# Two cross-attention blocks on one Trainium2 core: the last group's layer-1 probabilities turned by TensorE instead of VectorE and transfers

## What is computed

```python
q = (query @ Wq + bq).reshape(B, S, 16, 16).transpose(0, 2, 1, 3)
k = (key @ Wk + bk);  v = (value @ Wv + bv)          # one key/value head of 16
probs = softmax(where(|i - j| <= 64, q @ k.T * scale, NEG))
attn = (probs @ v) as (B, S, D) @ Wo + bo
gate = silu(concat([attn, query]) @ Wg + bg)
out = attn * gate + query * (1.0 - gate)
x_hat = out * rsqrt(mean(out * out, -1) + EPS) * rms_w
return x_hat - mean(x_hat, axis=1)
```

## Time and profile before

| | us |
|---|---|
| time, median of 3 runs (lowest to highest) | 1825.16 (1825.07 to 1828.34) |
| the profiled execution: its time | 1826.95 |
| the profiled execution: its span, first to last instruction | 1825.2 |
| PE busy in the span | 1792.8 (98%) |
| scores of group 31 start | 1785.96 |
| last `ag_sum` starts | 1813.90 |

### The profile page before, as it was taken

How to read it: one execution, slowest core, us unless ns; L and a number is a source line. 1 busy time by engine, 2 the same in 40 slices (tenths; PEclk the granted TensorE clock), 3 DMA queues, 4 the chain that set the end, 5 groups by cost and what they waited for, 6 DMA issues and landing times.

```text
span 1825.2 us, 55273 instructions
## 1 busy us (share of the span) xinstructions
PE 1792.8 (98%) x18702; PEld 1650.3 (90%) x18702; DVE 1485.3 (81%) x6755; ACT 1535.3 (84%) x5586; POOL 1292.3 (71%) x1324
## 2 busy tenths in 40 slices
PE   6999999999999999999999999999999999999997
PEld 5989999999999999999999999999999999999985
DVE  7878888888888888888888888888888888878775
ACT  5788888888889888889888889888888888888874
POOL 3656777767777766777766777776777776777754
PEclk9999999999999999999999999999999999999998
DMA  7434445444545544445544445444454444445432
GB/s 235 124 95 116 126 122 127 122 113 114 128 118 131 121 113 114 126 119 131 121 114 114 123 121 128 121 118 112 123 124 124 121 121 112 119 118 122 103 89 59
DMA packets 238059, 219.11 MB, mean 120 GB/s; under 512 B 48848, under 2 KB 220240, under 8 KB 237776
## 3 DMA queue, kind: packets, MB, share of 16 engines
q1 hardware_dynamic: 237776, 215.57, 47.2%
HBM read 71.29 MB, written 9.96 MB: 45 GB/s over the span
## 4 chain that ended last, share of the span: by engine, by line
PE 90%; DVE 4%; ACT 2%; POOL 1%; DMA 1%; issue 1%; SPq 0%; POOLq 0%; DVEq 0%; ACTq 0%
PE bank L616 11%; PE bank L618 11%; PE bank L617 11%; PE bank L630 9%; PE bank L634 8%; PE bank L631 8%; PE bank L790 7%; PE bank L803 7%; PE bank L915 4%; PE bank L928 3%; PE bank L626 3%; PE bank L622 3%; PE bank L623 3%; PE bank L640 2%; DVE soft L1754 1%
## 5 line engine op out<-in xcount | busy, mean ns | idle before, releaser
L2600 ACT ACTIVATE soft<-soft,row_min 128x128 f32<-128x128 f32 x1024 | 397.3, 392 | 60.9 <-DVE row_min L1754 60.8
L2520 ACT ACTIVATE soft<-soft,row_min 128x128 f32<-128x128 f32 x1024 | 398.5, 393 | 17.1 <-DVE row_min L1646 16.6
L3049 POOL TENSOR_TENSOR soft<-soft,inv_sum 128x512 f32<-128x512 f32 x256 | 271.4, 1061 | 145.7 <-DVE inv_sum L1654 145.7
L239 DVE STREAM_TRANSPOSE turned<-soft 128x512 f32<-128x512 f32 x512 | 341.8, 689 | 10.8 <-POOL soft L3058 4.7
L3058 POOL TENSOR_TENSOR soft<-soft,inv_sum 128x512 f32<-128x512 f32 x256 | 263.9, 1042 | 60.8 <-DVE inv_sum L1763 60.7
L1754 DVE CUSTOM_DVE_ANT_0 soft<-bank,winb 128x128 f32<-128x128 f32 x1024 | 230.3, 283 | 39.0 <-PE bank L915 36.3
L1646 DVE CUSTOM_DVE_ANT_0 soft<-bank,relb 128x128 f32<-128x128 f32 x1024 | 230.0, 281 | 15.3 <-PE bank L803 5.5
L2600 ACT ACTIVATION_READ_ACCUMULATOR soft<-soft,row_min 128x1 f32 x1024 | 195.2, 191 | 0.0
L2520 ACT ACTIVATION_READ_ACCUMULATOR soft<-soft,row_min 128x1 f32 x1024 | 195.0, 190 | 0.0
L790 PE MATMUL bank<-kT,qT 64*128 64x128 f32 x2048 | 148.7, 285 | 0.7 <-DVE kT L1626 0.7
L616 PE MATMUL bank<-wv,cT 128*128 128x256 f32 x512 | 146.5, 286 | 0.0
(11 more groups left out here) (249 smaller groups left out, 6448.5 us busy)
## 6 DMA issues: line engine op xcount, KB each, us to landing
soft<-turned SPq DMA_DIRECT2D x1024, 128.0 KB, 2.7
tokens<-stats_by_row SPq DMA_DIRECT2D x63, 256.0 KB, 3.6
tokens<-in_x SPq DMA_DIRECT2D x32, 256.0 KB, 2.8
raw<-in_x_t SPq DMA_DIRECT2D x32, 256.0 KB, 3.2
x<-in_x SPq DMA_DIRECT2D x32, 256.0 KB, 2.8
out<-gate SPq DMA_DIRECT2D x63, 128.0 KB, 2.5
tokens<-in_ctx SPq DMA_DIRECT2D x31, 256.0 KB, 2.9
raw<-in_ctx_t SPq DMA_DIRECT2D x31, 256.0 KB, 2.7
```

The lines of the kernel that those rows point to most:

```text
L239: return eng.transpose(turned[:, slot, :, s % 2, :, :].rearrange("p j h b -> p h j b"), soft[:, s, :, :].rearrange("p h (j a) -> p h j a", ...
L2520: last = act.activation(soft[:, s, h, :], soft[:, s, h, :], ACT.Exp, bias=row_min[:, s, h:h + 1], scale=-1.0, accum_out=row_sum[:, s, h:h ...
L2600: last = act.activation(soft[:, s, h, :], soft[:, s, h, :], ACT.Exp, bias=row_min[:, s, h:h + 1], scale=-1.0, accum_out=row_sum[:, s, h:h ...
L3049: pool.tensor_tensor(soft[:, m % NS0, :, :], soft[:, m % NS0, :, :], inv_sum[:, m % NS0, :].unsqueeze(2).broadcast_to([P, QUAD, SEQ]), ALU ...
```

## The change

Only group 31 (`g == NG - 1`) is touched. `norm1` writes its result into `turned`, with the keys in the order (a j) instead of (j a), so each write goes 16 bytes further than the one before, and no longer in place; for sequence 1 it waits until `turn_p` has read the same part for sequence 0. `turn_p` (PE) transposes the four heads of a unit with the identity into a bank; `place1` (DVE) copies the bank to the pair of slots, after both units of the pair are normalized. The eight `turn1` and the four `spread1` (16 transfers) go. PE's list is written anew with these calls in it, and other banks; `keep_busy` goes from 44 calls to 16 ahead of the turns and from 12 to 8 ahead of the last centering. `times_z`, `times_gate`, `plus_x` and `x_hat_lo` of sequence (31,1) go from POOL to DVE; `x_hat_lo(31,0)` on POOL moves ahead of `rrms_(31,1)`, and `y_out(31,0)` on DVE ahead of `x_hat(31,1)`.

```diff
@@ sync_program @@
-            spread1(NG - 1, 0, 0)
-            spread1(NG - 1, 0, 1)
-            spread1(NG - 1, 1, 0)
             store(NG - 2, 1)
-            spread1(NG - 1, 1, 1)
@@ tensor_program @@
+            def turn_p(g, b, u, bank, *drains):
+                freed(till, *drains)
+                till.wait_ge("norm1", unit1(g, b, u) + 1)
+                for h in range(QUAD):
+                    last = pe.transpose(bank[:, h * SEQ:(h + 1) * SEQ], in_key_order(u)[:, h, :], ident[:])
+                last.then_inc(sem["turn_p"], 1)
...
-                till.wait_ge(f"spread1_{n}", 16 * NB * (GROUP * g + b + 1))
+                if g == NG - 1:
+                    till.wait_ge("place1", NU1 * b + 2 * n + 2)
+                else:
+                    till.wait_ge(f"spread1_{n}", 16 * NB * (GROUP * g + b + 1))
...
-            keep_busy(banks[4], 44, ("min1", 8 * NG - 7))
...
+            keep_busy(banks[4], 16, ("min1", 8 * NG - 7))
+            turn_p(NG - 1, 0, 0, banks[4], ("min1", 8 * NG - 7))
+            turn_p(NG - 1, 0, 1, banks[1], ("min1", 8 * NG - 6))
+            pv1(NG - 1, 0, 0, banks[5], ("min1", 8 * NG - 3))
+            turn_p(NG - 1, 0, 2, banks[6], ("min1", 8 * NG - 5))
+            turn_p(NG - 1, 0, 3, banks[2], ("min1", 8 * NG - 4))
+            pv1(NG - 1, 0, 1, banks[5])
+            center_out(NG - 2, 1, banks[3], ("min1", 8 * NG - 2))
+            out_mm(NG - 1, 0, banks[7], ("min1", 8 * NG - 1))
+            turn_p(NG - 1, 1, 0, banks[4], ("place1", 1))
+            turn_p(NG - 1, 1, 1, banks[1], ("place1", 2))
+            out_mm_lo(NG - 1, 0, banks[7])
+            pv1(NG - 1, 1, 0, banks[0], ("min1", 8 * NG))
+            turn_p(NG - 1, 1, 2, banks[6], ("place1", 3))
+            turn_p(NG - 1, 1, 3, banks[2], ("place1", 4))
+            pv1(NG - 1, 1, 1, banks[0])
+            out_mm(NG - 1, 1, banks[4], ("place1", 5))
+            out_mm_lo(NG - 1, 1, banks[4])
+            keep_busy(banks[5], 8, ("o1_lo", 2 * NG - 1))
+            center_out(NG - 1, 0, banks[5], ("o1_lo", 2 * NG - 1))
+            center_out(NG - 1, 1, banks[3], ("y_out", 2 * NG - 2))
@@ vector_program @@
+            def place1(g, b, u, bank):
+                till.wait_ge("turn_p", NU1 * b + u + 1)
+                till.wait_ge("norm1", unit1(g, b, u | 1) + 1)
+                dve.tensor_copy(pair_of_slots(u // 2 if beside(g, b) else 2 + u // 2)[:, :, u % 2, :, :],
+                                bank[:].rearrange("p (h i b) -> p i h b", h=QUAD, i=NB)).then_inc(sem["place1"], 1)
...
-            turn1(NG - 1, 0, 0)
-            turn1(NG - 1, 0, 1)
+            place1(NG - 1, 0, 0, banks[4])
+            place1(NG - 1, 0, 1, banks[1])
             inv1(NG - 1, 0, 2)
             min1(NG - 1, 1, 1, banks[3])
             inv1(NG - 1, 0, 3)
             min1(NG - 1, 1, 2, banks[7])
-            turn1(NG - 1, 0, 2)
+            place1(NG - 1, 0, 2, banks[6])
             inv1(NG - 1, 1, 0)
-            turn1(NG - 1, 0, 3)
+            place1(NG - 1, 0, 3, banks[2])
             mean_sq(NG - 2, 1)
             min1(NG - 1, 1, 3, banks[0])
             inv1(NG - 1, 1, 1)
             x_hat(NG - 2, 1)
-            turn1(NG - 1, 1, 0)
-            turn1(NG - 1, 1, 1)
+            place1(NG - 1, 1, 0, banks[4])
+            place1(NG - 1, 1, 1, banks[1])
             inv1(NG - 1, 1, 2)
-            y_out(NG - 2, 1, banks[1])
+            y_out(NG - 2, 1, banks[3])
             inv1(NG - 1, 1, 3)
-            turn1(NG - 1, 1, 2)
-            turn1(NG - 1, 1, 3)
-            o1_lo(NG - 1, 0, banks[4])
-            ag_sum(NG - 1, 0, banks[6])
+            o1_lo(NG - 1, 0, banks[5])
+            place1(NG - 1, 1, 2, banks[6])
+            place1(NG - 1, 1, 3, banks[2])
+            ag_sum(NG - 1, 0, banks[7])
...
             gate_(NG - 1, 1)
+            times_z_last(NG - 1, 1)
+            times_gate_last(NG - 1, 1)
+            plus_x_last(NG - 1, 1)
             mean_sq(NG - 1, 1)
+            y_out(NG - 1, 0, banks[5])
             x_hat(NG - 1, 1)
-            y_out(NG - 1, 0, banks[3])
-            y_out(NG - 1, 1, banks[7])
+            x_hat_lo_last(NG - 1, 1)
+            y_out(NG - 1, 1, banks[3])
@@ gpsimd_program @@
+                if g == NG - 1:
+                    if b == 0:
+                        till.wait_ge(f"spread1_{u // 2}", 16 * NB * GROUP * g)
+                    else:
+                        till.wait_ge("turn_p", u + 1)
+                    pool.tensor_tensor(in_key_order(u).rearrange("p h (a j) -> p h j a", j=NB),
+                                       soft[:, s, :, :].rearrange("p h (j a) -> p h j a", j=NB),
+                                       inv_sum[:, s, :].unsqueeze(2).unsqueeze(3).broadcast_to([P, QUAD, NB, BLOCK]),
+                                       ALU.mult).then_inc(sem["norm1"], 1)
+                    return
...
             minus_x(NG - 1, 1)
-            times_z(NG - 1, 1)
-            times_gate(NG - 1, 1)
-            plus_x(NG - 1, 1)
+            x_hat_lo(NG - 1, 0)
             rrms_(NG - 1, 1)
-            x_hat_lo(NG - 1, 0)
-            x_hat_lo(NG - 1, 1)
```

More of the change, by code:

```diff
@@ L31 @@
         "cols_in", "consts_in", "raw0", "raw1", "raw2", "raw3", "raw4", "x_in", "tokens_in", "raw_in", "stat_out", "stat_in", "stored",
-        "keys_out", "keys_in", "spread0", "spread1_0", "spread1_1", "first_tokens", "first_raw", "first_out", "first_in")
+        "turn_p", "place1", "keys_out", "keys_in", "spread0", "spread1_0", "spread1_1", "first_tokens", "first_raw", "first_out", "first_in")
 def two_block_xattn(nc, t):
@@ L244, in pair_of_slots, with in_key_order @@
                 "p (i m h b) -> p i m h b", i=NB, m=2, h=QUAD)
+        def in_key_order(u):
+            return turned[:, 1 + u // 2, :, :, :, :].rearrange("p j m h b -> p (j m h b)")[
+                :, u % 2 * BANK:(u % 2 + 1) * BANK].rearrange("p (h n) -> p h n", h=QUAD)
         def spread(eng, pair, slot, name):
@@ L1797, in gate_, with times_z_last, times_gate_last, plus_x_last @@
                 dve.tensor_scalar(gate_of(g, b), gate_of(g, b), 0.5, 0.5, ALU.mult, ALU.add).then_inc(sem["gate"], 1)
+            def times_z_last(g, b):
+                till.wait_ge("gate", GROUP * g + b + 1)
+                till.wait_ge("times_z", GROUP * g + b)
+                dve.tensor_tensor(gate_of(g, b), gate_of(g, b), pre_gate_of(g, b), ALU.mult).then_inc(sem["times_z"], 1)
+            def times_gate_last(g, b):
+                till.wait_ge("minus_x", GROUP * g + b + 1)
+                till.wait_ge("times_z", GROUP * g + b + 1)
+                till.wait_ge("times_gate", GROUP * g + b)
+                dve.tensor_tensor(att_of(g, b), att_of(g, b), gate_of(g, b), ALU.mult).then_inc(sem["times_gate"], 1)
+            def plus_x_last(g, b):
+                till.wait_ge("times_gate", GROUP * g + b + 1)
+                till.wait_ge("plus_x", GROUP * g + b)
+                dve.tensor_tensor(att_of(g, b), att_of(g, b), x1[:, g % 2, b, :], ALU.add).then_inc(sem["plus_x"], 1)
+            def x_hat_lo_last(g, b):
+                till.wait_ge("x_hat_hi", GROUP * g + b + 1)
+                till.wait_ge("x_hat_lo", GROUP * g + b)
+                dve.tensor_tensor(flat(o1_of(g, b, LO)), att_of(g, b), f32(flat(o1_of(g, b, HI))), ALU.subtract).then_inc(
+                    sem["x_hat_lo"], 1)
             def mean_sq(g, b):
@@ L2438, in vector_program @@
             x_hat(NG - 2, 1)
-            turn1(NG - 1, 1, 0)
-            turn1(NG - 1, 1, 1)
+            place1(NG - 1, 1, 0, banks[4])
+            place1(NG - 1, 1, 1, banks[1])
             inv1(NG - 1, 1, 2)
-            y_out(NG - 2, 1, banks[1])
+            y_out(NG - 2, 1, banks[3])
             inv1(NG - 1, 1, 3)
-            turn1(NG - 1, 1, 2)
-            turn1(NG - 1, 1, 3)
-            o1_lo(NG - 1, 0, banks[4])
-            ag_sum(NG - 1, 0, banks[6])
+            o1_lo(NG - 1, 0, banks[5])
+            place1(NG - 1, 1, 2, banks[6])
+            place1(NG - 1, 1, 3, banks[2])
+            ag_sum(NG - 1, 0, banks[7])
             gate_(NG - 1, 0)
-            o1_lo(NG - 1, 1, banks[2])
+            o1_lo(NG - 1, 1, banks[0])
             mean_sq(NG - 1, 0)
-            ag_sum(NG - 1, 1, banks[5])
+            ag_sum(NG - 1, 1, banks[4])
             x_hat(NG - 1, 0)
             gate_(NG - 1, 1)
+            times_z_last(NG - 1, 1)
+            times_gate_last(NG - 1, 1)
+            plus_x_last(NG - 1, 1)
             mean_sq(NG - 1, 1)
+            y_out(NG - 1, 0, banks[5])
             x_hat(NG - 1, 1)
-            y_out(NG - 1, 0, banks[3])
-            y_out(NG - 1, 1, banks[7])
+            x_hat_lo_last(NG - 1, 1)
+            y_out(NG - 1, 1, banks[3])
         def scalar_program(act):
@@ L2992, in scalar_program @@
             exps1(NG - 1, 1, 3)
-            o1_hi(NG - 1, 0, banks[4])
+            o1_hi(NG - 1, 0, banks[5])
             tanh(NG - 1, 0)
-            o1_hi(NG - 1, 1, banks[2])
+            o1_hi(NG - 1, 1, banks[0])
```

## The result

The changed kernel is slower. In 17 runs each, its median is 1831.98 us (1829.15 to 1836.28) and that of the kernel before 1826.88 us (1824.60 to 1831.09); the ratio is 1.0032, 95% interval 1.0025 to 1.0039, that is 0.32% or 5.8 us (the two medians themselves differ by 5.1). The forecast was +2.3 us, inside what can't be told from no change. Its range ended at 1831.3, which is +6.1 counted from the 1825.16 that it started from; the kernel before came out 1.7 us above that here, so the difference lies near the upper end of the range and the time outside it. The profiled execution has a span of 1828.4 us.

A forecast was written before the change was run, and what follows sets the result against it. PE has 90% of the chain, but the change touches only the last 37 of 1825 us. Stages -0.05 + 4.0 - 0.1 - 1.8 = +2.1; forecast +2.3 on 1825.16, 1827.5 us, range 1824.2 to 1831.3.

The forecast's parts named there:

- stage B: Tail from out_mm(31,0) to ag_sum(31,0), which waits for PE: serial chain of 9.6 us where it was 5.53, +4.0.
- Stage A: Tail from the probabilities to out_mm(31,0)'s start: transfers' wait goes, ACT is late in its place, -0.5 to -0.05 us.
- `o1_hi(31,0)` released by ACT's own queue: Sign at the start of out_mm(31,0): ACT's queue, not PE, releases o1_hi(31,0), which ends at 1802.6 to 1803.05.
- With the low clock until about 1809.2: PE's clock in stage B: at 1.2 GHz until about 1809.2, making the serial chain 9.6 us, +4.0.
- the late return: PE's clock comes back only by 1812.6: stage B takes some 11.0 us, +5.4, and the whole sum is +3.5.
- Stage C: Tail from ag_sum(31,0) to ag_sum(31,1): same chain, 4.8 us before, 4.7 after; out_mm(31,1) late by 1.2 at the low clock.
- Stage D: Tail from ag_sum(31,1) to the end: products on DVE -0.8, x_hat(31,1) -0.5, x_hat_lo(31,1) -0.4, together -1.8 us.
- norm1's scattered write: norm1 on POOL writing 16 bytes apart: no row shows its cost; taken as 1.04 us, upper end 1.33.
- rival 3: norm1 takes 1.33 us for its scattered write: +3.9 us, or +4.3 with the clock's late return; chance 0.20.
- SP's queue needs 9.16 us to issue 12 transfers one after the other: Stage A: the transfers' wait before out_mm(31,0), removed by the change; at most 1.6 us to be had.
- rival 2: PE's clock still low at out_mm(31,1), with gaps of about 1.5 us after out_mm(31,0): +3.9 to +6 us; chance 0.16.
- Rival 4: The gain of all transfers arrives; no case reaches -3.65 us, since ACT stands right behind them; chance 0.05.

The follow-up runs named there:

- e6: Changed kernel with the last group's DVE, POOL and PE lists reordered and keep_busy calls filling PE's gaps; ratio to before 0.9953, tail 30.17 us.
- e10: The kernel before, unchanged, run again for a second trace; tail 35.71 us against 37.07 in the first.
- e9: The changed kernel, unaltered, run again for a second trace; tail 41.30 us against 42.25 in the first.
- e1: Changed kernel with 28 more keep_busy calls filling PE's gaps between turns and products; ratio to before 1.0006, tail 37.64 us.
- e2: Changed kernel with two turn_p of sequence (31,1) moved ahead of center_out(30,1) and out_mm(31,0); ratio to before 1.0005, tail 37.23 us.
- e5: Changed kernel with both two turn_p moved ahead of out_mm(31,0) and keep_busy calls in PE's gaps; ratio to before 0.9986, tail 34.73 us.
- e7: Kernel before, transfers kept, with the last gate products on DVE and keep_busy calls in PE's gaps; ratio to before 0.9994, tail 34.82 us.
- e4: Kernel before with only keep_busy cut as in the change (44 to 16 calls, 12 to 8); ratio 1.0002, tail 37.21 us.

## Why the prediction was wrong

Its four stages and its chain held. What failed is the size of stage B, through one term: the clock, which the prediction has back for good at a date read from the trace of before.

- **Stage A**: forecast -0.5 to -0.05, measured +0.26. The slip was as worked out: counted from the first exponential, `mean_sq(30,1)` is at 10.8 where it was 9.3, and `x_hat(30,1)` takes 1.07 us beside a `norm1` (0.46 in e6, where it starts 0.16 us ahead of the `norm1`, which then takes 1.29). But "`o1_hi(31,0)` released by ACT's own queue" was wrong: its row names `center_out(30,1)` (L979), for which it waits 0.32 us before it overwrites `o1T`. I had left that wait out.
- **Stage B**: forecast +4.0, measured +5.85. The serial chain was the right one, and its rows have the sizes used: `out_mm` 3.12 (3.15), two turns 1.91 (1.95), `place1` 0.69 (0.66). The failed step is "With the low clock until about 1809.2", which is 21.1 us after the first exponential. That date was carried over from before, where TensorE was full from 1803.5 on and had its clock back 5.6 us later, and e10 shows that not even before keeps to it (2.1). In the changed kernel it was full for 5.0 us, from 1801.85 to 1806.9, and then waited 1.57 us, and the clock stayed low until 31.9 us. Everything from `out_mm_lo` to the last turn then ran at 1.2 GHz: 1.22, 1.08 and 1.97 us, for which I had the high-clock prices. The prediction's own sum with the late return gives some 11.0, for 11.38 measured. In the second trace (e9) the return came at 20.6 us, close to the date assumed, and B was 10.03, close to the 9.6 of the sum; but the clock had fallen earlier (A 16.16) and fell again behind the 1.57 us gap (C 5.41). So it is not the date alone: the low clock was taken for one stretch that ends once, and in both traces it also covered `out_mm(31,1)`.
- **Stage C**: forecast -0.1, with +1.2 for `out_mm(31,1)` at the low clock; measured +0.72, since the clock came back just at its end (`out_mm_lo` took 0.62). The 1.7 us that the forecast has for `out_mm(31,1)` hangs on the same step.
- **Stage D**: forecast -1.8, measured -1.65. The products take 0.42 and not 0.36, and one of them twice that beside GpSimd.
- **norm1's scattered write**: 1.13 us in the median for 1.04, so nearly the price taken and not rival 3's 1.33. By the figure of the Trainium skill, GPSIMD Engine Reference, section "Performance pitfalls for Q7 kernels", taken over from reads to writes, it would have been about 1.5, as an estimate; the measurement decides, and the trace does not bear that transfer out.

Three smaller errors of the prediction change nothing in its forecast. "SP's queue needs 9.16 us to issue 12 transfers one after the other" misreads a merged row: the queue issues them in three groups of four, 2.5 us each, that start at 1794.45, 1797.52 and 1801.11, each 0.02 to 0.03 us after the end of a `turn1`. So the transfers followed VectorE and not the queue's own pace. The terms of the chain at the high clock add up to 7.3 and not 7.4 (e1 measured 7.65). And rival 3 "with the late return of the clock" is 3.5 + 1.8 = +5.3 by its own terms, not +4.3: that would have put the measured 5.8 near a rival which the trace rules out, as `norm1` took 1.13.

So what happened is rival 2, with +3.9 to +6 us, which I had given 0.16. Its text had the reason in it, TensorE's gaps behind `out_mm(31,0)`; I did not weigh it against the 5.6 us of full work that preceded the return in the only trace I had. e1, e2 and e5 show that the loss is the order, with its gaps, and the clock together. Rival 4's premise, that ScalarE stands right behind the transfers, does not hold for every order: e6 goes to 30.17 us with the same exponentials.

## What to carry to other kernels

A clock's return is not an event with a date that survives a change, or even a second execution (17.6 and 21.1 us after the exponential for the same kernel): price the stretch both with the clock back early and with it low throughout, and take the second seriously where gaps of waiting break TensorE's work up (here low for 20 us). When work moves from transfers to TensorE and VectorE it joins two in-order queues, so place it ahead of the long product that doesn't need it (here -5.0 us for moving two calls). A removed wait is worth what the next one leaves, and a bound like these transfers may show only when the rest is out of its way (e7).

## What the runs showed of the hardware that was not expected

- The clock fell 7.4 us after the first exponential in e4 and 14.2 in before, and the tail was the same within 0.14 us. The kernel before got it back after 5.6 us of full work in one execution and after 2.1 in another, for tails of 37.07 and 35.71 us. So a sum built on the return's date in one trace carries some 1.4 us of its own. The Trainium skill, TensorE: Matmul & The Clock Gate, section "What's actually happening", says that the monitor behind the clock runs freely and doesn't start with the kernel, so that the change-over lands at other places from run to run, by about half a microsecond either way. The two traces agree that it moves, but they are 3.5 us apart, and the measurement decides.
- An element-wise product or sum with both inputs in SBUF on VectorE took 0.78 to 0.83 us where a GpSimd operation was already running beside it and 0.42 where not, and `x_hat` 0.94 to 1.07 against 0.46 to 0.48. Where VectorE began first, GpSimd paid: 1.29 us for a `norm1` of 1.13 (e6).
- The start of the tail varied by 5.2 us between executions with the same work ahead of it, the whole size of the effect. What causes that was not looked into.
